# Second layer of a two-layer model on one core: projections and heads in one block, last feed-forward in two phases

## What is computed

```python
h = layernorm(x)                                # 1024 x 512
q, k, v = split(clip(h @ w_qkv.T, -8, 8))
q, k = layernorm(q) * wq + bq, layernorm(k) * wk + bk
# 32 heads of 16, causal, with a bias -slope[head] * distance
attn = softmax(mask(q @ k.T / 4 + alibi)) @ v
x = x + attn @ w_out.T
h = layernorm(x)
x = x + gelu(h @ w1 + b1) @ w2 + b2              # hidden width 2048
```

## Time and profile before

| | us |
|---|---|
| median of 3 runs (2048.13 to 2048.84) | 2048.5 |
| the profiled execution | 2049.02 |
| its span, first to last instruction | 2047.1 |
| attention projections, about | 1390 to 1491 |
| head stage | 1491 to 1803 |
| last feed-forward | 1832 to 2047 |

### The profile page before, as it was taken

One profiled execution on the slowest core, in us unless ns is written; L12 is line 12 of the kernel. 1 busy time (PEld: TensorE's weight loads), 2 busy tenths in 40 slices (PEclk: granted clock), 3 DMA queues, 4 the chain that ended last, 5 costly groups with the idle time before them and its releaser, 6 DMA issues. The chain is left out here.

```text
span 2047.1 us, 26945 instructions
## 1 busy us (share of the span) xinstructions
PE 1921.2 (94%) x10439; PEld 1508.9 (74%) x10439; DVE 856.7 (42%) x1586; ACT 436.7 (21%) x534; POOL 676.0 (33%) x816
## 2 busy tenths in 40 slices
PE   6999999999999999999999689998967999978998
PEld 4888888888888888888888578886733444356877
DVE  5242442432433424324324533305565888532332
ACT  3111111111121111111111020002303666631111
POOL 4322231311313222313100165436701221238765
PEclk9999999999999999999999889998966999988999
DMA  4010110110110101101100123102071333012333
GB/s 156 29 57 29 57 35 22 56 56 28 34 51 28 56 28 56 42 15 56 36 8 13 52 68 87 54 1 83 1 99 22 53 59 56 2 47 67 97 88 97
DMA packets 41124, 101.47 MB, mean 50 GB/s; under 512 B 7712, under 2 KB 12448, under 8 KB 36576
## 3 DMA queue, kind: packets, MB, share of 16 engines
q1 hardware_dynamic: 39784, 97.95, 16.5%
q10 hardware_dynamic: 1272, 2.61, 0.9%
HBM read 84.28 MB, written 2.10 MB: 42 GB/s over the span
## 5 line engine op out<-in xcount | busy, mean ns | idle before, releaser
L146 PE MATMUL a_ps<-a_xh_h,a_w_h 128*128 128x512 f32 x768 | 307.1, 400 | 3.4 <-POOL a_w_l L270 2.0
L148 PE MATMUL a_ps<-a_xh_h,a_w_l 128*128 128x512 f32 x768 | 301.1, 392 | 0.0
L147 PE MATMUL a_ps<-a_xh_l,a_w_h 128*128 128x512 f32 x768 | 300.3, 391 | 0.0
L60 POOL TENSOR_TENSOR tick<-neg_half 128x1 f32<-128x1 f32 x108 | 36.5, 338 | 659.9 <-PE a_ps L148 615.6
L390 DVE TENSOR_TENSOR x<-x,a_ps 128x1024 f32<-128x1024 f32 x64 | 78.2, 1222 | 260.0 <-PE a_ps L148 260.0
L1234 ACT ACTIVATE a1h_pr<-a1h_ps 128x1024 f32<-128x1024 f32 (+1 forms) x192 | 153.3, 812 | 92.4 <-PE a1h_ps L1364 71.2
L146 PEld LDWEIGHTS a_ps<-a_xh_h,a_w_h 128*128 128x128 f32 x768 | 144.8, 189 | 31.6 <-DVE a_xh_l L101 4.0
L148 PEld LDWEIGHTS a_ps<-a_xh_h,a_w_l 128*128 128x128 f32 x768 | 144.3, 188 | 30.3
L147 PEld LDWEIGHTS a_ps<-a_xh_l,a_w_h 128*128 128x128 f32 x768 | 144.8, 189 | 27.9
L1384 PE MATMUL a1h_ps<-a1h_KT,a1h_QT 64*128 64x512 f32 (+2 forms) x384 | 141.7, 466 | 24.9 <-DMA a1h_QT<-a_qslope 13.9
L1384 PEld LDWEIGHTS a1h_ps<-a1h_KT,a1h_QT 64*128 64x128 f32 x384 | 70.2, 205 | 98.8 <-DVE a1h_mx L1283 34.9
(11 more groups left out here) (189 smaller groups left out, 3819.5 us busy)
## 6 DMA issues: line engine op xcount, KB each, us to landing
a_raw<-in_a_wqkgv SPq DMA_DIRECT2D x30, 1024.0 KB
f_raw<-in_f_w SPq DMA_DIRECT2D x64, 256.0 KB, 2.6
f_raw<-in_f_w SPq DMA_DIRECT2D x33, 320.0 KB, 2.9
a_raw<-in_a_wout SPq DMA_DIRECT2D x32, 256.0 KB, 5.2
a_cst<-in_a_cst SPq DMA_DIRECT2D x32, 129.0 KB
a1h_KT<-a_k_h SPq DMA_DIRECT2D x64, 64.0 KB
a1q_raw<-in_a_wqkv SPq DMA_DIRECT2D x3, 1024.0 KB
a1h_QT<-a_q_h SPq DMA_DIRECT2D x40, 64.0 KB
```

The lines of the kernel that those rows point to most:

```text
L60: nc.gpsimd.tensor_tensor(top["tick"][:, :], top["neg_half"][:, 0:1], top["neg_half"][:, 1:2], ALU.mult)
L146: nc.tensor.matmul(out, w_hi, x_hi, start=start, stop=False)
L147: nc.tensor.matmul(out, w_hi, x_lo, start=False, stop=False)
L148: return nc.tensor.matmul(out, w_lo, x_hi, start=False, stop=stop)
```

## The change

**Projections and heads become one block.** `attention1_heads` has the projections in it; the tiles that only they need (`early`) lie at the same addresses as stacks and probabilities (`on_cl`, `on_raw`, `on_xh_h`, ...), so each stack of the first six pairs waits until what lay there has been used, and the meeting of all engines between the stages is gone. Within a tile m the first unit is turned after two of its four steps, the second at its end. Tiles 22 and 23 of v (m from `AFTER` on) go to banks 0 and 1, and their eight steps stand between the 24 pieces of pair 0, as `V_AT` says. The stacks are divided anew: ScalarE issues head 1 of K0, then K1, K2, and after the two casts Q3 to Q5; SyncE issues Q0, head 0 of K0, Q1, Q2, row 0, K3, row 1, K4, K5. VectorE clears the Q tiles one after another, the last three behind the eighth piece of pair 1.

**The last feed-forward has two phases**: all 32 units, whose hidden tiles are all kept (`h_h`, `h_l`), then the product with w2 for all eight token tiles in eight banks. Each weight tile is loaded and split once, written out without loops on the device. b2 is added one tile behind each of eight splits; layer norm tiles 4 to 7 are turned together between the first and the second unit.

```diff
@@ constants
+AFTER = 3 * NT - 2
+PROJ_BANK = [m % PROJ if m < AFTER else m - AFTER for m in range(3 * NT)]
+V_AT = {2 + 3 * i: (AFTER + i // KT, i % KT) for i in range(2 * KT)}
@@ stack
-            if kind and p < SETS:
-                queue.wait_ge(s("set_clear"), p + 1)
+            if p < SETS:
+                if kind:
+                    queue.wait_ge(s("set_clear"), p + 1)
+                elif p == 0:
+                    queue.wait_ge(qs("w_split"), 3 * KT)
+                elif p < 3:
+                    queue.wait_ge(qs("turned"), 12 if p == 1 else 16)
+                else:
+                    queue.wait_ge(qs("proj_done"), 3 * NT)
+                queue.wait_ge(qs("turned_lo"), 8 * (1 - kind) + 5 if p < 4 else 16)
@@ sync
-            stack(sp, 0, 0)
...
-            for p in range(1, SETS):
-                stack(sp, p, 0)
+            stack(sp, 0, 1)
+            stack(sp, 0, 0, (0,))
+            stack(sp, 1, 1)
+            stack(sp, 2, 1)
             max_row(0)
+            stack(sp, 3, 0)
             max_row(1)
+            stack(sp, 4, 0)
+            stack(sp, 5, 0)
@@ scalar
-            for p in range(SETS):
-                stack(act, p, 1)
+            stack(act, 0, 0, (1,))
+            stack(act, 1, 0)
+            stack(act, 2, 0)
             nc.scalar.copy(identb[:, :], ident[:, :]).then_inc(s("later_ready"), 1)
...
+            for p in range(3, SETS):
+                stack(act, p, 1)
+            act.wait_ge(qs("proj_done"), 3 * NT)
+            act.wait_ge(qs("turned_lo"), 16)
@@ vector
+                if m == QK - 1:
+                    dve.wait_ge(qs("w_split"), 3 * KT)
+                    clear(0)
+                if m == QK:
+                    dve.wait_ge(qs("turned"), 12)
+                    clear(1)
...
-            pieces(1, 2, NP)
+            pieces(1, 2, 8)
+            dve.wait_ge(qs("proj_done"), 3 * NT)
+            for i in range(3, SETS):
+                clear(i)
+            pieces(1, 8, NP)
@@ tensor
+                for k in range(KT):
+                    part(m, k)
+                    if k % 2:
+                        for u in between[k // 2:k // 2 + 1]:
+                            turn(u)
+            pe.wait_ge(qs("full"), 16)
+            pe.wait_ge(qs("clipped"), AFTER - 2)
             for k in range(NP):
                 piece(0, k)
+                if k in V_AT:
+                    part(*V_AT[k])
@@ stage_ffn1, tensor
+            hidden(0, 0)
+            ln_tensor(nc, pe, s, b, range(4, NT))
+            pe.wait_ge(s("ln_lo"), NT)
+            hidden(0, 1)
+            for f in range(1, NF1):
+                for half in range(2):
+                    hidden(f, half)
+            for f in range(NF1):
...
+                for t in range(NT):
...
+                    last = mm3(nc, ps[:, OUT[t], :], h_h[:, f, q], h_l[:, f, q], w_h[:, i, :], w_l[:, i, :],
+                               f == 0, f == NF1 - 1)
```

582 lines of the change are left out of this document (273 added, 309 removed).

## The result

| | before | after |
|---|---|---|
| median, us | 2048.3 (4 runs, 2046.4 to 2048.8) | 2024.5 (4 runs, 2022.1 to 2025.4) |
| profiled execution, us (span) | 2049.0 (2047.1) | 2025.4 (2023.7) |

The ratio is 0.9884, with a 95% interval of 0.9866 to 0.9901: faster by 24 us. The prediction was 2020.6, in a range of 2012.0 to 2029.5.

What follows compares the result with a forecast made beforehand. The prediction took matmuls as the feed-forward's limit, with gaps, and transfer issue as what TensorE awaits after the projections. Heads 12.0 plus feed-forward 15.9 made 27.9 off 2048.5: 2020.6 us, range 2012 to 2029.5.

Steps and rivals of the forecast that it cites:

- its own case: Whole kernel: the main forecast, 2017 to 2024 us, chance 0.50.
- Part 1: Projections: transposes between a tile's matmuls lengthen two TensorE waits; 2.2 us lost, bounds 0 and 2.8.
- Part 2: V tiles 22 and 23 among pair 0's maxima: VectorE covers them, 15.4 us; 4 more at low clock left out.
- Part 3: Stacks issued earlier and divided anew: ScalarE's 30 issues set the first exponential, 11.2 us earlier; 12.0 in all.
- Part 4: Quads of the heads: same instructions, left as they are; only the second exponential's 0.7 us won, counted beforehand.
- The meeting of the engines: End of the heads' block: no term was written; the stretch to the feed-forward's first transposes was forecast unchanged, 0.
- Part 5: Last feed-forward: two phases win 14.5 us, counting 2 for a lower clock; its tail wins 1.4; together 15.9.
- rival C: Feed-forward wins less: spacing 0.230, second clock fall, stores lining up, 5 us in all; 2025.6, chance 0.11.
- B: Less won before the quads: low clock makes TensorE pair 0's limit, 4 us, slower issues 1.8; 2026.4, chance 0.18.
- A: More won before the quads: faster issues (3.6), high clock in pair 0, earlier return in quad 0; about 2012, chance 0.17.
- D: Slower: the clock stays at 1.2 GHz beyond quad 0, up to 29 us more per later quad; chance 0.02.
- E: Nothing won: stacks land as late as before and the feed-forward's two phases stall on weights; 2048, chance 0.02.

Runs made afterwards that it cites:

- x_one_clear: Changed kernel with one set of semaphores in place of the second layer's two; median 2019.99 us, ratio 0.9859.
- x_three_behind: Changed kernel with one semaphore set, Q4 and Q5 issued by SyncE, early exponential table, and turns behind their tiles' matmuls; median 2012.2 us, ratio 0.9818.
- the four profiles named above: Changed kernel rerun, with old last feed-forward, with two hidden-unit banks, and with one semaphore set; first exponential 137.2 to 137.5 us into the block.
- x_issue_split: Changed kernel with stacks Q4 and Q5 issued by SyncE behind K5, leaving ScalarE only Q3 before the first exponential; median 2019.2 us, ratio 0.9856.
- x_table_early: Changed kernel with a one-column exponential on ScalarE ahead of Q3's issues, loading the table in idle time; median 2018.2 us, ratio 0.9844.
- x_ffn_only: Kernel before the change with only the new last feed-forward; 2032.5 us, ratio 0.9915.
- x_three_dense: Changed kernel with one semaphore set, Q4 and Q5 on SyncE, early table, and v portions behind every second maximum of pair 0; median 2012.0 us, ratio 0.9822.
- x_heads_only: Changed kernel with the old last feed-forward; 2037.5 us, ratio 0.9944.
- x_two_banks: Changed kernel with two PSUM banks in place of four for the last feed-forward's hidden units; median 2021.2 us, ratio 0.9865.
- x_three: Changed kernel with one semaphore set, Q4 and Q5 issued by SyncE, and the exponential's table loaded early; median 2010.1 us, ratio 0.9821.

## Why the prediction was right, and where it was off

The forecast of 2020.6 is 3.9 below the 2024.5, inside the range, and just outside the bracket of its own case (2017 to 2024). On the span 27.9 was forecast (its four terms as written, 11.2, 0.7, 14.5 and 1.4, make 27.8) and 23.4 measured: 3.1 and 3.05 that no term had, against 1.9 won beyond the forecast up to the last output copy. That the first layer's 3.05 and these 1.9 nearly cancel is luck, and so is part of the agreement within single parts below.

**Part 1, the turns (2.2 lost).** Right in sign and mechanism, mis-sized: the added waiting is 4.2, above the upper bound of 2.8. Turns wait at four places and not at two (1.58, 2.32, 1.46 and 3.38 in after). Of the two waits that I meant only the second grew beyond the 2.5 that I named as the limit. The net loss is 3.7 in after. That it is 2.1 in x_one_clear, as forecast, is luck: there the clock hands 1.6 back. I didn't see either that both profiles without the loss have the clock fall in pair 0, and the heads no faster.

**Part 2, the portions.** Right in the mechanism. VectorE covers them at the high clock, as x_one_clear's stretches show: pair 0 lasts 15.2 there, 15.4 forecast. The 4 us for a low clock all through were too little: with the clock at half from 3 us on (x_three_behind) the pair lasts 20.8, 5.6 more. The short dip of after cost 1.2.

**Part 3, the stacks.** The chain came in the order written, with 3.05 taken off for the later start: first maximum 1490.1 (1490 forecast), set 3 clear at 1511.8 (1512.3), last issue over at 1534.3 (1535.4), first exponential at 1535.7 (1536.7). The first of these is a hit by two errors: tile 21 ends at 1489.1, 1.8 later than forecast, and TensorE then waits 0.98 and not 2.7, since the first piece starts 2.1 behind ScalarE's last issue of the K stack and not 3.5. In the four profiles named above the first maximum is 1.6 earlier than in after and the rest 3 us. That ScalarE's issues set the end was argued; x_issue_split shows it. The Trainium skill's page ScalarE: Activation LUTs, section What ACT_TABLE_LOAD costs, adds 1380 ns for a drain to the load's 1283. Here the load takes the 1.28, ends at 1538.71, and the exponential starts at 1538.73; x_table_early gives back 1.3 and not 2.7. So this trace doesn't show the drain, and the sum was right to leave it out.

**Part 4, the quads (nothing but 0.7).** A term that I had seen and set to zero. From the first exponential to the last output copy it is 252.1 before, and 248.6 to 250.7 in the five profiles whose heads are as in the change or differ in the semaphores alone: 1.4 to 3.5 less, where I had 0.7. The same old heads in x_ffn_only take 254.6, where the clock came back 32 us behind the first exponential and not 23, so the size of this gain is known to some 2 us only. The first output copy comes 17.5 behind the first exponential in all five and 19.2 in both profiles of the old heads, so 1.7 is won at the very start, where two scores and the first pieces are already made; I had counted one exponential's wait of it. The two profiles at 248.6 have the clock at 1.00 from 180 to 380 us into the block; the three at 250.3 to 250.7 have 0.83 in the last 20 of these, and the other 1.8 goes with that.

**The meeting of the engines: the step that failed.** I costed what the change removes, one meeting between projections and heads, under the wait that it ended. I didn't ask what happens at the new block's end. There two sets of semaphores are now cleared one after the other, and nothing covers it: 2.64 us more idle time than before (4.61 against 1.97), and 0.57 more ahead of the feed-forward (5.40 against 4.83). x_one_clear takes both away with one line. Why a second set lengthens the later wait stays open. With this term, 3.1 by the stretch, the sum is 24.8 and the forecast 2023.7. It was there to be read: `ctx` closes two `Sems`, and the trace of before has a price for one, the idle 1.97 at 1803.26.

**Part 5, the feed-forward (14.5 and 1.4).** Right in the sum, 14.4 and 1.3, the second unit 10.5 behind the first (1834.52 to 1844.98; 10.6 forecast), no wait behind it. But two terms in it were off and cancelled. The 2 for a lower clock behind the second unit didn't come in after:

```profile
1845.00:1850.00 5.00, 5.00 (x22) 4.13 (x23) 2.30 (x4) 1.88 (x3) 1.73 (x2) 1.00 0.01 3
```

And from the second unit to the last matmul, 1844.98 to 2018.83, the 755 steps are 0.2303 each, not the 0.2275 of the earlier trace rows: 2.1 more, as rival C had it. The units have 0.2271, the product with w2 0.2333, so the missing 2 us lie in the second phase. The low clock was a fair fear: it came in three other profiles, x_one_clear, x_issue_split and x_three_dense, whose feed-forward takes 192.2 to 192.5, some 1 us longer. In x_one_clear behind the turns of tiles 4 to 7:

```profile
1838.32:1842.32 4.00, 3.64 (x10) 2.87 (x11) 1.42 (x3) 1.56 (x2) 0.00 (x0) 0.62 0.01 4
```

x_ffn_only and x_heads_only show that the feed-forward is independent of the heads, x_two_banks that the two further banks give none of it.

**The 3.05 of the first layer** were no part of the sum and rightly none, since the kernel with the old block shows such a difference too (1395.28 and 1399.56).

**Rivals.** B took place in part: a dip in pair 0 came in three of the eight profiles with turns and portions placed as in the change (after, x_table_early, x_three), in the other five not; it cost the pair 1.2, 2.2 and 2.3. The Trainium skill's TensorE: Matmul & The Clock Gate, section A second HAM failure mode, has the clock swing in groups with short idles that cycle through PSUM banks. The dips would fit that, but with the same groups five profiles have none, so no run here shows it to be the cause. Of A, the high clock through pair 0 came in those five; the early return of the clock in quad 0 came in x_three alone, with other edits. Of C the spacing took place, without making the feed-forward win less in after, since the 2 for the clock fell away there. D and E did not: the clock came back in every profile.

## What to carry to other kernels

When two blocks are made one, count what now happens at the end of the whole: every clearing of semaphores and every meeting that used to lie under some engine's wait may stand there uncovered, 2.76 us for the second one here, and one line takes it away. When a long row of transfer issues stands ahead of the first instruction that everybody waits for, leave on that engine only those that this instruction needs; the other queue took the rest in time that was free there, and the first exponential came 5.8 us earlier. And if an edit of some us is to be judged on a kernel whose single times move by as much, cut both traces at shared places and compare the pieces, and look at the granted clock in each piece before you lay a difference to the edit: in one pair of profiles the turns cost 3.7 us and in another 2.1, with the same waits.
